# Attention over blocks of eight heads by four keys, with the squares mixed on 64x32 tiles and the key blocks masked on GpSimd

## What is computed

```python
h = tok(x)                      # windows of 8 steps: softmax pooling, 750 -> 94 tokens of 64 channels
h = h + attn(layernorm(h))
h = h + ffn(layernorm(h))       # 16 routed experts and a shared one
...
# attn: 8 heads of 8 channels, n = m = 94 tokens
q, k, v = heads(x @ w_qkv.T + b_qkv)
qgr, _ = qr(q); kgr, _ = qr(k)
dots = einsum('bhnd,bhmd->bhnm', q, k)
a = concat([dots * scale, dots ** 2 * riem_scale, einsum(qgr, kgr) ** 2 * grassman_scale])   # 24 planes
a = (a - bn_mean) * inv + bn_beta
a = einsum('oc,bcnm->bonm', conv_w, a) + conv_b      # 24 planes -> 8 heads
a = softmax(a, axis=-1)
out = einsum('bhnm,bhmd->bhnd', a, v) @ w_proj.T + b_proj
```

## Time and profile before

| | us |
|---|---|
| median of 3 runs | 1020.79 (1018.34 to 1020.95) |
| the profiled execution | 1019.19 |
| its span, first to last instruction | 1017.5 |
| busy PE / DVE / POOL / ACT | 898.6 / 763.6 / 488.2 / 423.6 |

### The profile page before, as it was taken

The page is one execution under the profiler, slowest core; times in us unless marked ns, Lnnn a source line. Parts: engine busy times, 40 slices in busy tenths (PEclk is TensorE's granted clock), DMA queues, the critical chain, the costliest instruction groups (busy, mean ns, idle before and its releaser), DMA issues. The chain is left out here.

```text
span 1017.5 us, 37672 instructions
## 1 busy us (share of the span) xinstructions
PE 898.6 (88%) x15018; PEld 577.8 (57%) x15018; DVE 763.6 (75%) x1287; ACT 423.6 (42%) x710; POOL 488.2 (48%) x551
## 2 busy tenths in 40 slices
PE   3677668998937999999999999999999999799995
PEld 2233245555525666666666666666666666446663
DVE  4588863887983888888788888888888888747773
ACT  2333423112713444444444444444444444257774
POOL 3355631110007666666666666666666666212220
PEclk9777877998977999999999999999999999979998
DMA  8765000324102111111111111111111111001111
GB/s 300 263 223 202 1 0 1 55 54 115 31 0 64 50 49 50 52 52 52 48 45 48 50 52 52 52 49 46 48 49 50 52 52 53 2 3 29 29 29 32
DMA packets 64446, 63.25 MB, mean 62 GB/s; under 512 B 37081, under 2 KB 55068, under 8 KB 64412
## 3 DMA queue, kind: packets, MB, share of 16 engines
q1 hardware_dynamic: 63884, 61.25, 20.4%
q10 hardware_dynamic: 528, 1.54, 0.4%
HBM read 52.93 MB, written 6.75 MB: 59 GB/s over the span
## 5 line engine op out<-in xcount | busy, mean ns | idle before, releaser
L1163 ACT ACTIVATE sq<-ps_dot 128x752 f32<-128x752 f32 x192 | 153.1, 798 | 302.6 <-PE ps_dot L1042 302.6
L1042 PE MATMUL ps_dot<-q_st,k_blk 32*64 32x94 f32 x6144 | 169.4, 247 | 3.1 <-POOL k_blk L1002 3.1
L1042 PEld LDWEIGHTS ps_dot<-q_st,k_blk 32*64 32x64 f32 x6144 | 134.4, 133 | 64.6 <-issue 50.0
L1002 POOL TENSOR_TENSOR k_blk<-k_turn,hmask 128x384 f32<-128x384 f32 x64 | 65.3, 1020 | 177.8 <-ACT k_turn L1151 177.8
L1210 DVE TENSOR_REDUCE sums<-prob 128x94 f32<-128x564 f32 x128 | 148.0, 1201 | 2.0 <-ACT prob L1156 2.0
L1006 POOL TENSOR_TENSOR k_mix<-k_cm,cols 128x768 f32<-128x768 f32 x64 | 119.8, 1872 | 0.0
L988 POOL TENSOR_TENSOR v_blk<-v_rep,vmask 128x384 f32<-128x384 f32 x128 | 106.6, 854 | 6.8 <-PE ps_m L1074 6.8
L1091 PEld LDWEIGHTS ps_a<-q_st,k_mix 64*64 64x64 f32 x3072 | 77.1, 132 | 56.4 <-issue 48.2
L1091 PE MATMUL ps_a<-q_st,k_mix 64*64 64x94 f32 x3072 | 101.0, 250 | 0.8 <-DVE prob L1198 0.8
L1156 ACT ACTIVATE prob<-prob,cols 128x564 f32<-128x564 f32 x128 | 91.1, 758 | 20.4 <-DVE prob L1198 20.4
L1181 DVE TENSOR_REDUCE row_max<-ps_a 128x94 f32<-128x564 f32 x128 | 89.3, 741 | 12.4 <-PE ps_a L1110 12.4
(11 more groups left out here) (225 smaller groups left out, 1389.7 us busy)
## 6 DMA issues: line engine op xcount, KB each, us to landing
v_rep<-v_rows SPq DMA_DIRECT2D x256, 96.0 KB
x_g<-in_x_dram SPq DMA_DIRECT2D x15, 1500.0 KB, 6.7
v_rows<-tok SPq DMA_DIRECT2D x32, 96.0 KB
q_st<-q_cm SPq DMA_DIRECT2D x64, 47.0 KB
out_dram<-rows SPq DMA_DIRECT2D x16, 188.0 KB
x_g<-in_x_dram ACTq DMA_DIRECT2D x1, 1500.0 KB, 7.4
top_rows<-tok SPq DMA_DIRECT2D x16, 32.0 KB
top<-top_rows SPq DMA_DIRECT2D x1, 512.0 KB, 3.4
```

The costliest lines, as they stand in the source:

```text
L1002: return pool.tensor_tensor(k_blk[:, a, :, kind], view.unsqueeze(2).broadcast_to([128, NTAU, 4, 8]), k["hmask4"][:].unsqueeze(1).unsqueeze ...
L1042: mm = pe.matmul(ps_dot[64 * hg:64 * hg + 64, (a + g) % 2, b, col:col + N], k_blk[rows, a, 2 * (2 * g + t2) + mi].rearrange("p k h m -> p ...
L1163: act.activation(sq[:, :, :, 2 * g:2 * g + 2, :].rearrange("p mi b t n -> p b mi (t n)"), ps_dot[:, (a + g) % 2, :, 0:4 * N].rearrange("p ...
```

## The change

Keys are grouped by four with all eight heads in one block of 32 partitions (`SLOTS = 4` such blocks), where they were grouped by eight. What follows from it, in the parts of the program:

- `dots`: still 48 matmuls, now of 64 rows and 64 columns: one gives eight heads, four keys and both kinds. Its weights are every 24th element of `k_blk`. Results rotate over three PSUM banks instead of two pairs.
- POOL builds `k_blk` as all 96 keys times the head mask, 768 elements per kind instead of 384, in key order; `k_mix` in four instructions of 192 elements; `m_blk` two pairs ahead, and PE turns keys three pairs ahead.
- `mixing`: the squares of a pair are mixed by 16 matmuls of 64 rows by 32 columns over 282 columns. The 24 key products (`linear`) run before it.
- DVE: `sums_of` is replaced by `halves`, an addition of slots 0 to 2 and 3 to 5, between `maxima` and the head maxima; `denominators` adds the rest with six matmuls. The subtraction is in two instructions, by batch. The padding comes in through the bias of the exponential, so there are four exponentials; the squares are six instructions.
- `attended` is cut in two, one behind `dots(i, 0)` and one behind `dots(i, 1)`; `denominators` stands behind `spread_max`.
- The values go to DRAM with one DMA a chunk instead of two and are loaded with eight a pair instead of four.
- In `constants` two permutations are applied by matmuls, and POOL's `vmask` and `den_w` wait for their result.
- The steps of PE and the loads of SP are written out in place of loops.

The diff, cut to its core (where a removed line is not shown, it is in the functions above):

```diff
-        step(pool.tensor_copy(k["vmask"][:, t, :], k["hmask"][:]))
+        step(pool.tensor_copy(k["vmask"][:, t, :], moved[:, 0:8]))
     step(pool.tensor_tensor(k["den_w"][:].rearrange("p (o d) -> p o d", o=8),
-                            k["hmask"][:].unsqueeze(2).broadcast_to([128, 8, 8]),
+                            moved[:, 0:8].unsqueeze(2).broadcast_to([128, 8, 8]),
                             ones[:].unsqueeze(2).broadcast_to([128, 8, 8]), ALU.mult))
...
+    step(dve.tensor_copy(moved[:], ps_t[:, 1, 288:297]))
+    dve.sem_inc(heads_done, 1)
...
-    for quarter, source in enumerate((0, 2, 1, 3)):
-        mm = pe.matmul(ps_t[32 * quarter:32 * quarter + 32, 1, 256:320], k["ident"][:, 32 * source:32 * source + 32], mix_rows[:],
-                       start=True, stop=True)
-    mm.then_inc(pe_step, 1)
+    pe.matmul(ps_t[:, 1, 256:288], key_order[:], mix_rows[:], start=True, stop=True)
+    pe.matmul(ps_t[:, 1, 288:297], head_order[:], moving[:], start=True, stop=True).then_inc(pe_step, 1)
...
-        for mi in range(2):
-            sp.dma_start(v_dram[bass.ds(c * 2 * CP, 2 * CP), mi].rearrange("b j f -> j b f"),
-                         tok[mi:96:2, a].rearrange("p r b f -> p (r b) f")[:, :, 128:192]).then_inc(stored[a], 16)
+        sp.dma_start(v_dram[bass.ds(c * 2 * CP, 2 * CP)].rearrange("b j f -> j b f"),
+                     tok[:, a].rearrange("p r b f -> p (r b) f")[:, :, 128:192]).then_inc(stored[a], 16)
...
-k_blk = sb("k_blk", [128, 2, NTAU, 2, 4, 8])
-k_mix = sb("k_mix", [128, 2, NTAU, H, 8])
+k_blk = sb("k_blk", [128, 2, 2 * H * NP])
+k_mix = sb("k_mix", [128, 2, NT, SLOTS, H, 4])
...
-sq = sb("sq", [128, 2, 2, NT, N])
+sq = sb("sq", [128, 2, SLOTS, 3, N])
...
+half = sb("half", [128, 2, 3, N])
...
+ps_dot = ctx.enter_context(nc.psum_tensor("ps_dot", [128, 3, 512], F32))
+ps_a = ctx.enter_context(nc.psum_tensor("ps_a", [128, 4, 512], F32))
...
+            src = v_dram[span(2 * i + b, 1)].rearrange("b (m c t) f -> c m (b t f)", c=SLOTS, t=NT)
+            for c in range(SLOTS):
+                sp.dma_start(v_rep[32 * c:32 * c + 32, a, b, :], src[c].unsqueeze(0).broadcast_to([H, 4, NT * C])).then_inc(v_in[a], 16)
+    for i in range(PAIRS):
+        load(i, i % 2)
...
+    def turning(i, a):
+        if later(i, 2):
+            pool.wait_ge(s["kt_done"], i - 1)
         pool.tensor_tensor(m_blk[:, a], m_t[:, span(i, 1), :].broadcast_to([128, 16, D]),
                            k["mask16"][:].unsqueeze(2).broadcast_to([128, 16, D]), ALU.mult).then_inc(s["m_ready"], 1)
+    def blocked(a, kind, keys):
+        at = kind * H * NP
+        return pool.tensor_tensor(k_blk[:, a, at:at + H * NP].rearrange("p (h m) -> p h m", h=H), keys.unsqueeze(1).broadcast_to([128, H, NP]),
+                                  k["hmask"][:].unsqueeze(2).broadcast_to([128, H, NP]), ALU.mult)
+    def build(i, a, n, has_next2):
+        if has_next2:
+            turning(i + 2, a)
         if later(i, 2):
...
+            pool.wait_ge(s["keyed"], 2 * (i - 1))
+        keys = k_cm[:, span(i, 1), :].rearrange("p i (m c t) -> p c (i t) m", c=SLOTS, t=NT)
+        for c in range(SLOTS):
+            mix = pool.tensor_tensor(k_mix[:, a, :, c], keys[:, c].unsqueeze(2).broadcast_to([128, NT, H, 4]),
+                                     k["conv1"].unsqueeze(1).unsqueeze(3).broadcast_to([128, NT, H, 4]), ALU.mult)
+        mix.then_inc(s["mix_ready"], 1)
+        blocked(a, 0, k_cm[:, span(i, 1), :].rearrange("p i m -> p (i m)")).then_inc(s["keys_ready"], 1)
         pool.wait_ge(s["kt_out"], i + 1)
...
+        blocked(a, 1, k_turn[:, a, :]).then_inc(s["keys_ready"], 1)
...
-        for t2 in range(2):
-            for mi in range(2):
+            pe.wait_ge(q_in[a], of_parity(i, a, 16) + 16)
+            pe.wait_ge(s["keys_ready"], 2 * i + 2)
+            pe.wait_ge(s["kt_out"], min(i + 3, PAIRS) if isinstance(i, int) else i + 3)
+        if g or later(i, 1):
+            pe.wait_ge(s["squared"], 6 * i + (-1, 1, 3)[g])
+        for c in range(SLOTS):
+            for v in range(2):
                 for b in range(2):
-                    for hg in range(2):
-                        rows = slice(64 * b + 32 * hg, 64 * b + 32 * hg + 32)
-                        col = N * (2 * mi + t2)
-                        mm = pe.matmul(ps_dot[64 * hg:64 * hg + 64, (a + g) % 2, b, col:col + N],
-                                       k_blk[rows, a, 2 * (2 * g + t2) + mi].rearrange("p k h m -> p (k h m)"),
-                                       q_st[rows, a, :], start=True, stop=True)
+                    rows = slice(64 * b, 64 * b + 64)
+                    mm = pe.matmul(ps_dot[64 * v:64 * v + 64, (2 * g + b) % 3, N * c:N * c + N],
+                                   k_blk[rows, a, 6 * c + 3 * v + g:2 * H * NP:NP // 4], q_st[rows, a, :], start=True, stop=True)
...
+    def attended(j, a, slots):
+        if slots[0] == 0:
+            pe.wait_ge(s["exp_done"], 2 * j + 2)
+            pe.wait_ge(s["v_ready"], j + 1)
+            if later(j, 1):
+                pe.wait_ge(s["out_done"], j)
+        for t in slots:
+            for b in range(2):
+                pe.matmul(ps_m[64 * b:64 * b + 64, AV_AT:AV_AT + N], v_blk[:, a, b, t, :], prob[:, a, b, t, :],
+                          start=(t == 0), stop=(t == NT - 1), skip_group_check=True)
+    def denominators(j):
+        pe.wait_ge(s["half_done"], j + 1)
+        for t in range(3):
+            for b in range(2):
+                mm = pe.matmul(ps_m[64 * b:64 * b + 64, DEN_AT:DEN_AT + N], k["den_w"][:], half[:, b, t, :],
+                               start=(t == 0), stop=(t == 2), skip_group_check=True)
+        mm.then_inc(s["av_done"], 1)
+    def linear(i, a):
+        if later(i, 1):
+            pe.wait_ge(s["sub_done"], 2 * i)
+        pe.wait_ge(s["mix_ready"], i + 1)
         for t in range(NT):
             for b in range(2):
...
+                for w in range(2):
+                    half_of = slice(64 * w, 64 * w + 64)
+                    mm = pe.matmul(ps_a[half_of, 2 * b + t // 3, N * (t % 3):N * (t % 3) + N],
+                                   k_mix[64 * b:64 * b + 64, a, t, 2 * w:2 * w + 2].rearrange("p c o m -> p (c o m)"), q_st[64 * b:64 * b + 64, a, :],
+                                   start=(t % 3 == 0), stop=False, skip_group_check=True)
+                if t == NT - 1:
+                    mm.then_inc(s["keyed"], 1)
+    def squares_mixed(i, b, v):
+        for c in range(SLOTS):
+            mm = pe.matmul(ps_a[32 * c:32 * c + 32, 2 * b + v, 0:3 * N], k["mix_w"][64 * v:64 * v + 64, :],
+                           sq[64 * v:64 * v + 64, b, c].rearrange("p t n -> p (t n)"), start=False, stop=True, skip_group_check=True)
         return mm
...
+    def mixing(i):
+        pe.wait_ge(s["squared"], 6 * i + 5)
+        squares_mixed(i, 0, 0)
+        pe.wait_ge(s["keyed"], 2 * i + 1)
+        squares_mixed(i, 0, 1).then_inc(s["mixed"], 1)
+        pe.wait_ge(s["squared"], 6 * i + 6)
+        squares_mixed(i, 1, 1)
+        pe.wait_ge(s["keyed"], 2 * i + 2)
+        squares_mixed(i, 1, 0).then_inc(s["mixed"], 1)
+    def step(i, a, has_prev, has_prev2, has_next3):
         dots(i, a, 0)
+        if has_prev2:
+            attended(i - 2, a, (0, 1, 2))
         if has_prev:
             turn_max(i - 1)
         dots(i, a, 1)
+        if has_prev2:
+            attended(i - 2, a, (3, 4, 5))
         if has_prev:
             spread_max(i - 1)
+        if has_prev2:
+            denominators(i - 2)
         dots(i, a, 2)
...
+        if has_next3:
+            turn_keys(i + 3, 1 - a, 0, 6 * i + 4)
+        linear(i, a)
+        mixing(i)
+    for i in range(3):
+        turn_keys(i, i % 2, i, None)
+    for i in range(PAIRS):
...
+            act.wait_ge(s["keys_ready"], 2 * (i - 1))
+        act.activation(k_turn[:, a, :], ps_dot[:, bank, KT_AT:KT_AT + NP], ACT.Copy).then_inc(s["kt_out"], 1)
+    def exps(prev, a, b):
+        act.wait_ge(s["sub_done"], 2 * prev + b + 1)
+        act.activation(prob[:, a, b, 0:4], prob[:, a, b, 0:4], ACT.Exp, bias=k["head_const"][:])
+        act.activation(prob[:, a, b, 4:6], prob[:, a, b, 4:6], ACT.Exp, bias=k["pad_bias"][:]).then_inc(s["exp_done"], 1)
+    def squares(i, g):
+        act.wait_ge(s["dots_done"], 3 * i + g + 1)
         for b in range(2):
...
+            act.activation(sq[:, b, :, g, :], ps_dot[:, (2 * g + b) % 3, 0:SLOTS * N].rearrange("p (c n) -> p c n", c=SLOTS),
+                           ACT.Square).then_inc(s["squared"], 1)
+    def step(i, a, has_prev, has_prev2, has_next3):
         if has_prev:
...
+            act.wait_ge(s["mixed"], 2 * i)
+        squares(i, 0)
+        squares(i, 1)
+        if has_prev:
+            exps(i - 1, 1 - a, 0)
+        squares(i, 2)
+        if has_next3:
+            turned_out(i + 3, 1 - a, 0)
+        if has_prev:
+            exps(i - 1, 1 - a, 1)
...
+    def halves(j, a):
+        dve.wait_ge(s["exp_done"], 2 * j + 2)
+        if later(j, 1):
```

(29 more changed lines are left out.)

227 lines of the change are left out of this document (69 added, 158 removed).

## The result

The changed kernel takes 1085.74 us (median of 4 runs, 1084.03 to 1086.99) against 1020.53 before: ratio 1.0642, interval 1.0619 to 1.0665. That is 65 us slower, where 1011 with a range of 970 to 1080 was forecast. What happened is rival (b), POOL's turn between the two copies, at a smaller price than the 1104 us written there; and the weights with a step cost more than was taken. Times are medians of the fast executions; one of e12_pieces, 1053.00 us at a mean granted clock of 0.88 where its others have 0.93 to 0.94, is in a slower state of the chip and left out.

What follows compares the result with a forecast made beforehand. TensorE's queue was taken to set the attention step of 8.86 us; with DVE's copies waiting for POOL it becomes 8.70: 1019.2 + 64 x (8.70 - 8.86) + 2 = 1011 us, own range 1001 to 1018, wide range 970 to 1080.

Steps and rivals of the forecast that it cites:

- rival (b): POOL gets its turn between DVE's two copies; spread_max at 5.3, step 10.15, 1104 us; chance 0.20.
- the 4.1: Attention step: the forecast is wrong if spread_max starts before 3.5 or after 4.1 us of a step.
- the two copies wait to 3.4 and end at 3.8: DVE's copies of the head maxima wait for POOL's k_blk; spread_max at 3.85 instead of 3.74, step 8.7 us.
- The strided weights: Dots weights read with a step of 24 elements: +0.25 us a group, bounds 0 to 0.43, dots 1.06.
- Mixing: TensorE's 16 matmuls on the squares: two rounds, 1.12 us, with the wait for the keyed count 1.23.
- Attended and denominators: TensorE, three pieces of six matmuls, each followed by a tile-shape change: 0.61 us each, 1.83 in all, +0.54.
- DVE's chain behind spread_max: From spread_max to the key products: shift, two subtractions of about 0.75 us, hand-overs; 2.42 us.
- TensorE's work beside it: TensorE's own work from spread_max to the key products: 0.31 + 0.61 + 1.06 + 0.39 = 2.37 us.
- POOL in all: POOL's busy time in an attention step: 5.9 + 0.54 + 0.9 = 7.3 us, up to 8.1.
- the 0.1 for a change of tile shape: TensorE's attended and denominators: 0.1 us a change, an estimate with bounds 0 and 0.2.
- rival (a): Attention step: weights at full rate and DVE never behind POOL; step 8.09, 972 us; chance 0.20.
- vmask and den_w standing bare: Constants stage: both wait for its last matmul and stand bare at its end; +2 us, bounds 0 and 3.

Runs made afterwards that it cites:

- e12_pieces: Changed kernel with each of POOL's two key blocks built by four instructions of 192 elements instead of one of 768: 1027.61 us, ratio 1.0068 to the kernel before.
- e1_one_copy: Changed kernel with DVE's two copies of the head maxima made one copy of 256 elements: 1024.99 us, ratio 1.0068 to the kernel before.
- e2_psum_source: Changed kernel with row_max_o, the source of DVE's two copies, in PSUM instead of SBUF: 1025.46 us, ratio 1.0063 to the kernel before.
- e9_filler: Changed kernel with dots weights read side by side (other dot products than the reference's) and 12 more matmuls in front of spread_max: 1073.59 us.
- e7_side_psum: Changed kernel with k_blk laid out so the 64 dots weights lie side by side, and DVE's two copies reading from PSUM: 964.48 us, ratio 0.9478.

## Why the prediction was wrong, by its own steps

**The step that failed.** "the two copies wait to 3.4 and end at 3.8. Spread_max at 3.85 instead of 3.74: step 8.7." The first copy did as written (its wait ended at 3.44, the copy at 3.52). The second did not follow it: POOL's next key block took the turn, the copies ended at 4.95 and spread_max came at 5.01, past the 4.1 that the prediction had set as a sign of its being wrong. That is rival (b), which I put at 5.3. What spoke against it there was misread. The 0.36 for both copies in the earlier trace rows, begun at 604.86, falls into POOL's idle time. POOL in the same step of the kernel before:

```profile
602.82 1.89 POOL L1006 TENSOR_TENSOR k_mix<-k_cm,cols 128x768 f32<-128x768 f32 x1
607.54 1.02 POOL L1002 TENSOR_TENSOR k_blk<-k_turn,hmask 128x384 f32<-128x384 f32 x1 [2.83 <-ACT k_turn L1151]
```

It stood still from 604.71 to 607.54. In the one held pair, it was the same: behind k_mix, which ended at 320.10, POOL waited for k_turn and began its next instruction at 322.64, so the second copy was free to follow. The prediction itself says that the change ends that idle time, and did not draw from it that the old pair of copies stopped being a model. Price: e1_one_copy and e2_psum_source both take it away and both give 1025, so 0.97 us a step, 61 us of the 1086.

**The term that was mis-sized.** The strided weights: taken at +0.25 a group, measured 1.20 - 0.81 = +0.39, near the upper bound of 0.43. One step of its working did not hold: the 107 ns by which a stepped load of 128 columns was longer were halved to 54 for 64 columns, but a load of 64 columns with that same step of 8 is 216 - 136 = 80 ns longer, and with the step of 24 it is 223 - 133 = 90. Over three groups that is 0.42 a step more than forecast. Once the copies are free, stride and all, TensorE is full at 8.91, and the kernel is 0.7% slower than before, not 0.9% faster. The stride's price with free copies is 8.91 - 7.90 = 1.01 a step, 1025 - 964 = 61 us (three times 0.39 less 0.16, because behind spread_max DVE's 2.32 stays). While the copies are held it is only 0.23 a step (9.88 against the 9.65 of e9_filler), 12 us, since TensorE waits anyway. So two costs of 61 us each stood on a saving of 56 us (7.90 against 8.88 a step). The stride alone would have cost about what the change saves.

**What held.** Mixing 1.23 forecast, 1.21 measured. Key products 1.20, measured 1.13. Attended and denominators three times 0.61, measured 0.64. Turn_max 0.40, measured 0.35. DVE's chain behind spread_max 2.42, measured 2.32 where it sets the pace. TensorE's work beside it 2.37, measured 2.54, which decides in the changed kernel and is longer through the stride. POOL in all 7.3 a step, measured 7.80 with its wait for the halves, and ACT 5.2, measured 4.39. k_blk 1.47, measured 1.46; a k_mix piece 0.60, measured 0.63 with its overlap; the halves about 0.75, measured 0.73 free and 1.14 with their wait. One of these was luck in part: the 0.1 for a change of tile shape, which the 0.61 rests on, had no row. With the forecast's own terms and no stall or stride the step was 8.09, rival (a)'s 972 us; e7_side_psum reached 7.90 and 964.5.

**Outside the attention.** Forecast +2 us for vmask and den_w standing bare. The pooling stage does begin 2.4 us later, but nothing of it is left at its end (142.27 against 142.39), so as a part of the whole this term was nothing. Counted by the spans of the two traces, 1082.3 - 1017.5 = 64.8: the attention stage begins 0.7 earlier; from there to the first dots it takes 3.1 more, with two more pairs' keys turned and the wait for k_turn, which the forecast did not have; the first two steps take 1.1 more, the other 61 steps up to the last dots(0) 61.0 more, and what comes after 0.3 more. The stages in front of the attention differ by more than the term between traces whose code is the same there: over the eleven traces of the changed kernel and its variants the attention begins between 304.5 and 309.9 us, and no run shows why. So times of whole runs are compared here together with their steps.

**The range.** 970 to 1080 ended 6 us under the measured time, because (b) with 0.20 was left out whole and priced at 1104.
